# Attention of four layers on one core: the PV products move from behind the turns of P to before them

## The reference

```python
sim = jnp.einsum('bhij,bjd->bhid', ...)          # q (4,16,512,64) with one k (4,513,64)
sim = sim + attn_bias                            # (16, 512, 513), the first key is the "null" key
sim = jnp.where(causal, neg, sim)                # key j only for query i >= j - 1
sim = jnp.where(m, sim, neg)                     # padding mask
attn = jax.nn.softmax(sim, axis=-1)
out = jnp.einsum('bhij,bjd->bhid', attn, v)      # P times V
out = out.transpose(0, 2, 1, 3).reshape(b, n, HEADS * DIM_HEAD)
return ln(out @ Wout, g_out)
```

## Time and profile before

| what | value |
|---|---|
| median of 3 runs | 2241.24 us (2236.04 to 2244.11) |
| the profiled execution, its own time | 2235.24 us |
| its span | 2233.5 us |
| mean granted TensorE clock | 0.941 of full speed |
| PE busy | 1989.6 us (89%), 15859 instructions |
| PE weight loads busy | 1412.1 us (63%) |
| DVE busy | 1108.1 us (50%) |
| ACT busy | 982.1 us (44%) |
| POOL busy | 560.6 us (25%) |
| attention of layer 0 | from 103.9 us (first score) to 350.8 us (end of the last `put_out`) |
| attention of layer 1 | first score at 560.0 us |
| attention of layer 3 | first score at 1615.0 us |

### The profile page before, as it was taken

One profiled execution on the slowest core, in us unless ns is written; L12 is line 12 of the kernel. 1 busy time (PEld: TensorE's weight loads), 2 busy tenths in 40 slices (PEclk: granted clock), 3 DMA queues, 4 the chain that ended last, 5 costly groups with the idle time before them and its releaser, 6 DMA issues. The chain is left out here.

```text
span 2233.5 us, 44588 instructions
## 1 busy us (share of the span) xinstructions
PE 1989.6 (89%) x15859; PEld 1412.1 (63%) x15859; DVE 1108.1 (50%) x3360; ACT 982.1 (44%) x2572; POOL 560.6 (25%) x872
## 2 busy tenths in 40 slices
PE   6899999988899999699978876978799999969995
PEld 3477777745677777466655655864477777736663
DVE  5388882265788833200015544118588882421113
ACT  2388882145788832111112331214588882212221
POOL 2022220057111113411115333116611111421111
PEclk9999999989899999799988986998999999979997
DMA  2185523000644220333222654530010004131113
GB/s 86 34 238 160 163 82 100 0 1 1 193 116 116 59 77 34 104 110 108 99 85 76 171 166 133 198 133 9 19 33 22 21 12 152 53 122 48 45 43 125
DMA packets 158555, 197.80 MB, mean 89 GB/s; under 512 B 15443, under 2 KB 132143, under 8 KB 158349
## 3 DMA queue, kind: packets, MB, share of 16 engines
q1 hardware_dynamic: 146732, 168.83, 25.2%
q0 software_dynamic: 11616, 26.26, 3.3%
HBM read 120.33 MB, written 88.64 MB: 94 GB/s over the span
## 5 line engine op out<-in xcount | busy, mean ns | idle before, releaser
L1006 ACT ACTIVATE att_pr<-all_h,att_nmax 128x128 f32<-128x128 f32 (+3 forms) x768 | 420.9, 551 | 52.7 <-DVE att_nmax L959 52.7
L1070 PEld LDWEIGHTS att_t_ps<-all_ident,att_pr 64*128 64x128 f32 x3840 | 164.1, 139 | 105.2 <-issue 48.4
L1266 PE MATMUL out_y_ps<-outw_wo,mem_qt 128*128 128x256 f32 x768 | 180.2, 389 | 0.0
L1070 PE MATMUL att_t_ps<-all_ident,att_pr 64*128 64x64 f32 x3840 | 170.5, 224 | 10.6 <-DVE att_pt L968 10.6
L1940 PE MATMUL exp_f_h_ps<-exp_f_xs_t,cw_f_w 128*128 128x512 f32 (+1 forms) x512 | 173.3, 498 | 1.5 <-DVE exp_f_xs_t L1978 1.5
L1952 PE MATMUL exp_f_y_ps<-cw_f_w,exp_f_hid 128*128 128x256 f32 x768 | 168.4, 379 | 0.0
L968 DVE COPY att_pt<-att_t_ps 128x1024 f32<-128x1024 f32 (+2 forms) x168 | 166.4, 990 | 0.0
L1266 PEld LDWEIGHTS out_y_ps<-outw_wo,mem_qt 128*128 128x128 f32 x768 | 145.6, 194 | 25.3 <-issue 6.2
L2008 ACT ACTIVATE exp_f_hid<-exp_f_h_ps 128x512 f32<-128x512 f32 (+1 forms) x128 | 62.4, 490 | 217.1 <-PE exp_f_h_ps L1940 217.1
L1952 PEld LDWEIGHTS exp_f_y_ps<-cw_f_w,exp_f_hid 128*128 128x128 f32 x768 | 144.8, 190 | 19.5 <-issue 0.5
L959 DVE CUSTOM_DVE_ANT_0 all_h<-att_s_ps,att_bias,mem1k_nsn 128x128 f32<-128x128 f32 (+3 forms) x256 | 128.2, 547 | 36.4 <-PE att_s_ps L1053 26.7
(11 more groups left out here) (393 smaller groups left out, 3626.9 us busy)
## 6 DMA issues: line engine op xcount, KB each, us to landing
sorted_c<-all_zero SPq DMA_DIRECT2D x8, 2056.0 KB, 13.9
sorted_f<-all_zero SPq DMA_DIRECT2D x8, 2056.0 KB, 12.0
cw_f_w<-in_L_ffn_w_dram SPq DMA_DIRECT2D x16, 1024.0 KB, 8.0
cw_f_w<-in_L_ffn_W_dram SPq DMA_DIRECT2D x12, 1024.0 KB, 7.4
band<-rev SPq DMA_DIRECT2D x2, 4096.0 KB, 19.0
att_bias<-band SPq DMA_DIRECT2D x32, 256.0 KB, 3.0
com_f_rows<-expert_f SPq DMA_DIRECT2D x16, 512.0 KB, 6.0
tw_f_wab<-in_L_ffn_w_dram SPq DMA_DIRECT2D x2, 4096.0 KB, 19.8
```

Of the source, the lines that this page charges most:

```text
L1006: nc.scalar.activation(pr[u % 4][:, hh, at], sc[u % 4][:, hh, at], ACT.Exp, scale=-1.0, bias=nmax[:, b + k, q, h:h + 1], accum_out=rsum[:, ...
L1070: last = nc.tensor.transpose(t_ps[e % 2][:, half, (q + 1) * (n * hh + k) + kb, :], pr[u % 4][d, hh, at:at + P], c.ident[d, d])
L1266: nc.tensor.matmul(y_ps[b % 2][:, q, :], c.out_t[:, p, P * at:P * (at + 1)], wo[:, p, :], start=(p == 0), stop=False)
```

## The change

In each step of TensorE's loop, `values(u - 4)` is issued right behind `scores(u + 2)`, and `turn(u - 1)` and `turn_sums` come after it. Nothing else is edited.

```diff
@@ -1101,12 +1101,12 @@
             for u in range(NU + 4):
                 if u + 2 < NU:
                     scores(u + 2)
+                if u >= 4:
+                    values(u - 4)
                 if 1 <= u <= NU:
                     turn(u - 1)
                 if u - 3 in group_after:
                     turn_sums(group_after[u - 3])
-                if u >= 4:
-                    values(u - 4)
```

## The result

The changed kernel takes 2250.46 us (median of 7 runs, 2248.77 to 2254.42), the kernel before 2240.33 us in runs of the same session (7 runs). The ratio is 1.0051, with a 95% interval of 1.0036 to 1.0067: about 11 us slower (8 to 15). (The ratio is not the quotient of the two medians, which is 1.0045, or 10 us.) Its profiled execution has a span of 2248.6 us, 15.1 more than that of before.

A forecast was written before the change was run, and what follows sets the result against it. TensorE was taken to set the pace nearly everywhere. Per pair 0.74 us more, 6.0 us a layer, +18 us in three layers on the profiled 2235.24 gives 2253, or 2259 us for the median; range 2236 to 2277.

The forecast's parts named there:

- Price of a step: Undisturbed TensorE step: 2.48 us instead of 2.43, +0.05, as turns behind a gap lack first weights loaded ahead.
- The first rival: TensorE, scores to PV: PV's weights load while scores stream, so a step takes 2.33 us; faster, 2232 us; chance 0.13.
- The rival that called the 0.05 nothing: TensorE's steps: equal numbers of changes cost the same, only waits move; about +1.6 us a layer, 2246 us; chance 0.22.
- The wait for the copy: Unit 7's step: turns' wait for VectorE's copy, 0.67 us per pair, goes; unit 1's 0.09 likewise.
- The first PV and `put_out`: Unit 8's step: PV waits for `put_out`, giving back the 0.67 us and costing 0.23 us more per pair.
- The other groups: First PV of q = 1 waits 0.15 us for `put_out`; nothing of the kind for the two remaining groups.
- What comes later: Turns up to 1.1 us later in their step delay ScalarE's and VectorE's copies and the exponentials; costed at nothing.
- The fourth case: VectorE's late copies of units 5 and 7 delay `largest` and scores: 14 us on top, 2273 us; chance 0.15.
- Ends: Layer's end: last turns come behind a PV waiting for `put_out`, 0.4 us per layer; POOL passed by nothing.

The follow-up runs named there:

- all steps but units 7 and 8's: Kernel before with PV ahead of the turns in every step except those issuing the scores of units 7 and 8: 2250.22 us, ratio 1.0050.
- an earlier `put_out`: Changed kernel with `put_out` of q = 0 moved between the two heads of `largest` of unit 7, and POOL's `select` ahead of `null_less_max`: 2236.47 us, ratio 1.0006.
- units 7 and 1: Kernel before with PV ahead of the turns only in the steps issuing the scores of units 7 and 1: ratio 0.9923, run again 0.9936.

## Why the prediction was right

It said slower, 2259 us, within 2236 to 2277; measured were 2250.5. The mechanism is the one forecast; the sum was too large by 7 us (18 forecast, 11 measured, of an interval that reaches 15). Put into the prediction's own sum, the terms that the timelines give make 8 x 0.21 + 7 x 0.36 + 0.14 + 1.08 = 5.4 us a layer, 16 in three, where it had 6.0 and 18. So the steady part was right to 2 us, and by two errors against each other: the pairs were put 4 us too high, the ends 2 us too low. In the profiled executions the three attentions differ by 14.3 us, in large part because the starts of the layers were 1.3 us shorter. The rest down to the 11 us of the medians lies in no row that I can name.

- *Price of a step.* Forecast 2.48 us for an undisturbed step of q = 2; measured 2.48 (188.46 to 190.94). Scores to PV, of which there was no row, took 0.90 us, 0.91 forecast: the switch costs 0.09, as from turns to PV. The first rival (PV's weights load while scores stream) is out: PV's first load starts with PV, at 189.36, behind 0.55 us without a load. But the prediction's argument against it, that PV's weights take all rows, proves too much. Among PV products, which take all rows too, loads do overlap products: the 16 loads of 0.13 to 0.14 us each lie within 0.85 us, and from the third on they start while PV products stream. Across a change of rows, either way, no load ran ahead in the steps read here. The rival that called the 0.05 nothing is out as well; all steps but units 7 and 8's show it at 1.0050. The drain rule of the Trainium skill, TensorEngine Tiling (Array Packing), "Key Properties", fits the trace as far as the count goes: both orders change the rows in use twice per step. By the count alone the 0.05 would be 0, and the trace has it: it is the first weights of the turns, which are no longer loaded ahead behind PV (the rows of PEld above); 16 turns take 0.55 to the next 64-row product (190.39 to 190.94) against 0.50.
- *The wait for the copy.* Forecast gone; gone. Turning unit 7's step round alone is worth 0.32 us a pair.
- *The first PV and `put_out`.* Forecast: PV at 0.15 us behind `put_out`, unit 6 to unit 9 8.17 us; measured 0.14 and 8.15. Shown from both sides, by the old order in that step alone (7.61) and by an earlier `put_out` (7.57; POOL's `select` was moved with it, but with units 7 and 1 it made no difference whether it was, 7.52 and 7.51). The profile counts 0.52 us of waiting there, where I had written some 0.7.
- *The other groups.* Unit 0's step takes 2.44 us (196.02 to 198.46), 2.30 before: 0.14 with the 0.05 in it, where 0.20 was forecast. Its PV waited 0.09 (0.74 behind the scores where 0.65 would do), forecast 0.15; and that 0.15 had left out the 0.15 from the end of `put_out` to PV which the prediction counts in unit 8's step, so it was near by luck. Unit 1's step takes 2.11 (198.46 to 200.57), 2.20 before: -0.09, where -0.04 was forecast. **These terms were mis-sized.** I took 0.09 for unit 1's wait; the turns behind that wait had also lost the first weights (0.52 us to PV in 197.75 to 198.27, where 12 turns that do not wait take 0.47, 340.35 to 340.82), so turning round cost that step no second time. The seven other steps lose 0.04 to 0.05 each, 0.31 together, where 0.35 was forecast. A pair is 0.57 longer, 0.74 forecast, 4 us in 24 pairs.
- *What comes later.* Forecast at nothing. VectorE waits 17.6 us for turns in layer 0 and ScalarE 20.0, where ScalarE had 12.1 and VectorE none; no score waits for `largest` in the steady part but those of unit 8's second head, 0.2 us, which were forecast. The fourth case, VectorE as the bound, is out.
- *Ends.* **Forecast 0.4 us a layer, measured 1.08** (11.68 against 10.60). I followed one wait at the end, the 0.44 us of the earlier trace rows; before has one more, of 0.19. In the changed kernel the two are 0.58 and 0.43, and a third has come, of the last sums for POOL's `spread`, behind turns, a copy and an `invert` that are all later; the prediction had POOL passed by nothing. It made up for 2 us of the error in the pairs:

```profile
353.82 0.47 PE L1081 MATMUL att_t_ps<-all_ident,att_rexp 64*128 64x64 f32 x8 [0.49 <-POOL att_rexp L926]
```

- *The start of layer 0* (first score to scores of unit 6) is 0.4 us shorter in the changed kernel, 15.90 against 16.31, mostly in steps whose order is the same. That is no effect of the change that could be told: the two executions of the kernel with 7 and 1 have 16.29 and 15.85.

## What to carry to other kernels

Filling an engine's wait with other work is worth only as much as that work's own waits allow: look at what the moved work waits for, and at who waits behind it. Here the same swap gained 0.4% in one step of twelve and lost 0.5% in all, for two reasons: in the next step it put PV, which waits for the longest chain, ahead of the turns that had hidden this wait (0.54 us a pair), and in the ten other steps, where there was next to nothing to fill, it cost mostly 0.04 to 0.05 us each (0.34 a pair) and 1.08 us at each end. So turn round the one step that waits, not the loop. And count changes between kinds of products in the cycle, not in the step: scores, PV, turns has as many as scores, turns, PV. What differed was who had its first weights loaded ahead.

## What the runs showed of the hardware

- Turns behind scores, both over 64 rows, start without a gap: in unit 8's step of the kernel before 0.82 us after the masks (214.35 to 215.17), 0.17 for the masks and two times 0.32 for the products. Their first weights are loaded 0.32 us ahead. A change between 64 and 128 rows costs 0.09 us either way, as the single records of the trace show, in which products start in pairs: score products start 0.32 apart, PV 0.41 behind the last of them; turns 0.06 apart, PV 0.15 behind the last; PV products 0.11 apart, turns 0.20 behind the last. Turns that come behind PV or behind a wait take 0.05 us more: their second pair starts 0.11 behind the first, not 0.06.
- Where the scores of one step wait for the bank of their second head, the step loses less than the stop is long. In the run with unit 7 alone the two masks of unit 8 start 0.25 us apart (212.04 and 212.29) and not together; the turns come after 1.00 us (213.04), 0.82 without a stop, so 0.18 later.
- A releaser named by a trace can be wrong. VectorE's timeline of the kernel before shows a wait ahead of `largest` of unit 8:

```profile
215.47 0.62 DVE L959 CUSTOM_DVE_ANT_0 all_h<-att_s_ps,att_bias,mem0k_nsn 128x384 f32<-128x384 f32 x1 [0.18 <-POOL att_bias L910]
```

I took it for a real wait for POOL and moved POOL's `select` for it. Leaving POOL alone later cost nothing (7.51 us from unit 6 to unit 9 against 7.52), while moving it had cost 1.5 us once.
